# Attention inside a macaron block: maxima ahead of scores in the first half of each group of three turns, behind them in the second, with projections and transposes at other places in the order

## The reference

```
x = x + 0.5 * ffn(layernorm(x))
x = x + attention(layernorm(x))
x = x + 0.5 * ffn(layernorm(x))

ffn(x):        8 routed experts (top 2, normalized sigmoid gates) and one shared one,
               each gelu(x @ W1 + b1) @ W2 + b2, hidden size 128
attention(x):  its own layernorm with scale and bias gives h
               c_q = h @ w_down_q.T      c_kv = h @ w_down_kv.T      (128 wide)
               q, k, v = up-projections of c_q, c_kv, c_kv: 16 heads of 64
               rotary embedding on all 64 dimensions of q and k
               out = softmax(q k.T / 8) v @ w_out.T + x
```

## Time and profile before

| | |
|---|---|
| Median of 3 runs | 4095.67 us (4092.33 to 4099.59) |
| Profiled execution, its own time | 4098.04 us |
| Span in the profile | 4096.1 us, mean granted TensorE clock 0.988 |
| TensorE busy | 3897.4 us, 95% |
| GpSimd busy | 2932.8 us, 72% |
| VectorE busy | 2849.5 us, 70% |
| ScalarE busy | 2536.2 us, 62% |

### The profile page before, as it was taken

One profiled execution on the slowest core, in us unless ns is written; L12 is line 12 of the kernel. 1 busy time (PEld: TensorE's weight loads), 2 busy tenths in 40 slices (PEclk: granted clock), 3 DMA queues, 4 the chain that ended last, 5 costly groups with the idle time before them and its releaser, 6 DMA issues. The chain is left out here.

```text
span 4096.1 us, 65749 instructions
## 1 busy us (share of the span) xinstructions
PE 3897.4 (95%) x24908; PEld 2207.7 (54%) x24908; DVE 2849.5 (70%) x3796; ACT 2536.2 (62%) x3191; POOL 2932.8 (72%) x1632
## 2 busy tenths in 40 slices
PE   7999979999999999999999999999999999989999
PEld 6888834444444444444444444444444444478888
DVE  5656567777777776777778777767776777565563
ACT  4455446766766676667666766766676666645544
POOL 3444448878877897888788878878887888634443
PEclk9999989999999999999999999999999999999999
DMA  3233221111211221121122212211211121142331
GB/s 123 99 124 109 81 93 53 60 55 59 83 53 53 71 66 53 61 81 53 53 66 76 63 53 66 68 50 60 86 55 53 58 79 62 33 145 76 125 114 63
DMA packets 192772, 300.36 MB, mean 73 GB/s; under 512 B 50328, under 2 KB 100937, under 8 KB 191817
## 3 DMA queue, kind: packets, MB, share of 16 engines
q1 hardware_dynamic: 192456, 296.17, 22.3%
HBM read 201.20 MB, written 26.73 MB: 56 GB/s over the span
## 5 line engine op out<-in xcount | busy, mean ns | idle before, releaser
L1088 DVE TENSOR_REDUCE atNM<-atPS 128x2 f32<-128x1024 f32 x1024 | 1225.7, 1219 | 452.8 <-PE atPS L899 450.1
L1029 ACT ACTIVATE atPT<-atPS 128x1024 f32<-128x1024 f32 x1024 | 1014.0, 1024 | 773.1 <-PE atPS L920 766.7
L1187 POOL TENSOR_TENSOR atACC<-atACC,atPT 128x1024 f32<-128x1024 f32 x510 | 1238.7, 2429 | 89.3 <-ACT atPT L1029 39.1
L931 PE MATMUL atPO<-atPT,atV 128*64 128x512 f32 x4096 | 1014.2, 602 | 0.0
L1187 POOL TENSOR_TENSOR atACC<-atPT 128x1024 f32<-128x1024 f32 x255 | 606.6, 2379 | 262.8 <-PE atOT L953 181.7
L1020 ACT ACTIVATE atPS<-atSH 128x1024 f32<-128x1024 f32 x683 | 687.4, 1023 | 50.8 <-DVE atNM L1088 34.0
L920 PE MATMUL atPS<-atQH,atKL 64*128 64x512 f32 x2048 | 459.9, 445 | 66.3 <-DVE atPS L1094 51.7
L931 PEld LDWEIGHTS atPO<-atPT,atV 128*64 128x64 f32 x4096 | 259.0, 136 | 456.5 <-issue 433.1
L899 PE MATMUL atPS<-atKH,atQH 64*128 64x512 f32 x2048 | 444.0, 431 | 10.0 <-ACT atQH L1009 7.9
L1094 DVE COPY atPS<-atSH 128x1024 f32<-128x1024 f32 x341 | 418.7, 1228 | 37.9 <-DMA atSH<-atMD 11.4
L920 PE MATMUL atPS<-atQH,atKH 64*128 64x512 f32 x2048 | 406.6, 393 | 0.0
(11 more groups left out here) (278 smaller groups left out, 6461.5 us busy)
## 6 DMA issues: line engine op xcount, KB each, us to landing
atSH<-atMD SPq DMA_DIRECT2D x128, 512.0 KB, 4.3
atVT<-atR SPq DMA_DIRECT2D x508, 128.0 KB, 2.1
f1GB<-f1GD SPq DMA_DIRECT2D x128, 256.0 KB, 6.7
f2GB<-f2GD SPq DMA_DIRECT2D x128, 256.0 KB, 6.8
atRSUM<-atRD SPq DMA_DIRECT2D x126, 256.0 KB, 4.0
X<-x SPq DMA_DIRECT2D x4, 1024.0 KB, 6.0
XS<-x SPq DMA_DIRECT2D x16, 256.0 KB, 3.6
x<-X SPq DMA_DIRECT2D x16, 256.0 KB, 2.3
```

The lines of the kernel that those rows point to most:

```text
L931: ins = pe.eng.matmul(PO[HI[h], :], V[n % 2][:, j, HI[h]], PT[k % NPT][:, h, :], start=j == 0, stop=j == T - 1)
L1029: act.eng.activation(PT[k % NPT][:, :, :], PS[ring.of[step]][:, :, :], ACT.Exp, scale=SCALE).then_inc(grown.sem)
L1088: dve.eng.tensor_reduce(NM[:, q // 4, :, q % 4, t], PS[ring.of[step]][:, :, :], AX.X, ALU.max, negate=True).then_inc(most_out.sem)
L1187: pool.eng.tensor_tensor(total[:, :, :], begun[:, :, :], PT[k % NPT][:, :, :], ALU.add).then_inc(gathered.sem)
```

## The change

The order is written otherwise, in four respects; no instruction is added or taken away.

1. In the first half the maximum of turn x comes ahead of the score of turn x; in the second half the score of turn x+2 comes ahead of the maxima of turns x+1 and x+2. By TensorE's blocks: score, maximum, score and maximum, score, maximum become maximum, score, score and score, maximum, maximum. The ring of banks still gives each score the bank of the same maximum as before.
2. Where the side steps of turn x hold no other use of TensorE (`uses` is empty), those of turn x+1 are taken into the first half too, ahead of its attends.
3. Where turn x+1 has a `raise` and turn x+2 has another use, `apart` puts the steps of turn x+2 into the raise's place, ahead of the attends, and the raise behind the attends. That meets the raise of turn 4 with the sum of turn 5 (group 3), and in some batches a raise with a transpose or with the row of turn 11.
4. The transposes and latents of the second half of a batch's tokens stand at other periods (`TURNS`): transposes on turns 7 and 9 and not on 14 and 15, latents on 15 and 1 and not on 0 and 1.

```
-            TURNS = [(-21, late), (-20, late), (-17, early), (-17, late), (-9, early), (-9, late), (-8, early), (-8, late)]
+            TURNS = [(-21, late), (-20, late), (-17, early), (-17, late), (-13, late), (-12, late), (-9, late), (-8, late)]
...
+            def uses(steps):
+
+                return [s for s in steps if s[0] in ("turn", "latent", "raise", "value", "row", "sum", "outward")]
+
+            def apart(one, two):
+
+                raised = [s for s in one if s[0] == "raise"]
+                if raised and uses(two):
+                    return [s for s in one if s not in raised] + two, raised
+                return one, two
...
             for x in range(-42, 2 * PER * (NN + 4), 3):
-                order += tile("score", x) + most_of(x) + tile("fill", x + 2) + tile("score", x + 1)
-                order += others_of(x) + held + tile("attend", x - 1)
-                order += gathers(held + tile("attend", x - 1))
-                order += most_of(x + 1) + tile("score", x + 2) + most_of(x + 2)
+                order += most_of(x) + tile("fill", x + 2) + tile("score", x) + tile("score", x + 1)
+                now, some, more = held + tile("attend", x - 1), others_of(x), []
+                if not uses(some):
+                    more = others_of(x + 1)
+                order += some + more + now + gathers(now)
+                order += tile("score", x + 2) + most_of(x + 1) + most_of(x + 2)
                 now, held = tile("attend", x), tile("attend", x + 1)
                 if x % T < T - 1:
                     now, held = now + held, []
-                order += tile("fill", x + 3) + others_of(x + 1) + tile("fill", x + 4) + now + gathers(now) + others_of(x + 2)
+                one, two = apart(others_of(x + 1), others_of(x + 2))
+                order += tile("fill", x + 3) + one + tile("fill", x + 4) + now + gathers(now) + two
```

## The result

The changed kernel takes 4132.65 us (median of 4 runs, 4131.02 to 4133.29), the one before took 4097.14 beside it (4 runs, 4092.33 to 4099.59). The ratio is 1.0088, with a 95% interval of 1.007 to 1.0105. The forecast was 4099 with a range of 4065 to 4132, and slower was its likeliest sign at 0.40. The time lies at the range's upper edge, 0.65 us outside, and 34 us from the forecast. The profiled execution has a span of 4129.1 us, 33.0 more than before.

What follows compares the result with a forecast made beforehand. TensorE, 95% busy, was taken as the bound, with only its idle time to win. Losses of 5.5 and gains of 4.8 us per 96 turns gave +7.5, edit 4 -5, together +2.5: 4099 us, range 4065 to 4132.

Steps and rivals of the forecast that it cites:

- The sum for the hand-followed chains: Attention's two half-group chains, each group type followed once: 5.5 us lost, 4.8 won in 96 turns, +7.5 us in all.
- with `qlow` as in the row: Group 3: `qlow` taken at 1.9 to 2.2 us, group then 9.0 instead of 10.34, gain put at 1.1 each.
- the second rival: Group 3's `qlow` caught inside a GpSimd gather, 3.0 us each, and group 1's delaying group 4: +26, 4125; chance 0.14.
- -0.7 for each of the 7 batches, -5 in all: Edit 4's moved transposes: fewer waits behind `outward` (12.4 us), less ScalarE's copies and raises behind; between -12.4 and +5.
- B: Start of a group's third score, from which the second half's times are counted; 1818.56 in the group 7 followed.
- The loss list of 5.5 in 96 turns: Groups 7 (1.4), 2 and 10 (1.4), 11 (0.8), 13 without `outward` (0.5), smaller pieces in seven groups (1.4).
- the gains of 4.8: Per 96 turns: group 3 2.2 us, first halves with one attend and free VectorE (14, 15, 0, 1) 2.6.
- Only the gains come: Rival: second half's fill ready as before, losses of groups 7, 13, 2, 10 more than halved; 4062, chance 0.18.
- Bare second halves cost more than their row: Rival: ScalarE's own steps ahead of the late fill cost groups 12, 9, 5, 6, 8 0.3 each; +32, 4131; chance 0.13.
- the 20 that would have proved the sum wrong: Sign: score waits on ScalarE's fill rise from 12.8 to over 40 us; staying under 20 would disprove the sum.

## Why the prediction was wrong

**The sum for the hand-followed chains held in most of its parts.** It had 5.5 us lost and 4.8 won in 96 turns, +7.5 us in all; the groups without a transpose show +14.5, and group 3 below is 5 of the 7 between. Its largest losses are there by size: group 7 0.67 each (forecast 0.7), groups 2 and 10 0.25 to 0.45 (0.35), group 11 0.38 (0.4), group 13 without `outward` 0.42 (0.5). Of the gains, group 14 has 0.87, group 0 with `outward` 0.93, groups 1 and 15 0.48 and 0.47, as forecast (0.4 to 0.9). Group 1 with `outward` loses 0.22 and the other group 15 0.52, against 0.15 to 0.35.

**Group 3 was over-sized.** Its 1.1 each would be 23 us over 21 groups; the traces show 17.9. The step that failed is "with `qlow` as in the row". `qlow` did not stay at 1.9 to 2.2 but rose from a median of 1.93 to 2.69 in these groups. In them the changed kernel's group 3 takes 9.57 us with a `qlow` of 2.69, 9.78 with 2.90 and 10.05 with 3.17: what `qlow` takes more, the group takes more, and carried down to the 2.19 of the forecast the same line gives 9.07 for its 9.0.

The Trainium skill (page "SBUF — State Buffer", section "Who interferes with whom") says that only the port pair which VectorE and GpSimd share makes them contend, as an exclusive lock. The traces agree. In the kernel before and in the changed one `qlow` takes 1.21 to 1.22 us when it meets no gather. When it starts more than 0.15 us before the end of a gather, it ends 1.08 to 1.09 us behind that end, in all 39 and 38 cases. The other way round holds too: a gather that starts inside `qlow` ends 2.2 to 2.3 us behind `qlow`'s end, where a gather alone takes 2.38. So the length of `qlow` is the rest of a gather and 1.08, and moving it ahead inside the gather could win nothing.

That is the second rival's mechanism, and it happened, at less than its price. Its sign was the median of all 64 `qlow`, over 2.4 us; that median is 1.657 us (1.716 before), because the longer `qlow` is in group 3 and in a few of the groups 1. Its second part is there as well. In three of 21 pairs `qlow` in group 1 rose from 1.22 to 3.0 us, and the group 4 behind each is 1.45 to 1.49 us longer than before.

**The step that made the miss is edit 4's, "-0.7 for each of the 7 batches, -5 in all".** The groups with transposes show +16.1 instead: 21 of the 30.5 us by which the span missed the forecast of +2.5. It priced edit 4's transposes, with the copy HT and the raise behind it, and what it priced was about right: 5.4 us by the rows, and 7.5 in the run where no row is moved. What it put at nothing is the `row` of turn 11, which edit 3 also moves, in the four groups 9 that have a transpose on turn 9. My text names it in the change and no sentence of the sum costs it. Those four groups are 15.6 of the 16.1. Two of them would be there without edit 4, two are its doing, which is why undoing edit 4 changed the time by 1.4 us only. The price of such a row could be had from the chain that the prediction had already written down: the reductions end at B + 3.60 and the next use can start at B + 1.36, which is 2.24 us with nothing left to run, and `minus` (0.16) behind them makes 2.40. It was 2.39, four times, and behind three of them the clock took some 1.5 us more each (4.1 to 4.4 against 2.7). Letting the row stay behind gave 10.4 us back.

**The second half's order costs more than the losses that were listed, and the rest gains less.** The loss list of 5.5 in 96 turns is 59 us, the gains of 4.8 are 51. Undoing the second half's order gave back 56.8 us in the groups without a transpose and 15.4 in the others, 79.6 in all by the medians; the rest of the change is worth 44. So the near-cancelling sum stood for two large effects, both real, and neither is the list that was written. Group 7's loss, 15 of the 59, was mostly edit 2's (0.49 of 0.67 by the run that leaves it out there), and groups 14 and 4 would have won more with the old order (0.69 and 0.65). That 59 and 51 stand near 80 and 44 is luck in part.

**The other rivals.** "Only the gains come" needed the first maximum of a second half reduced within 0.7 us of the score's start; its reduction starts at 1.24. "Bare second halves cost more than their row" gives 4131, next to the measured time, and that is a coincidence. It asks for 0.3 us more in each of groups 5, 6, 8, 9 and 12; their medians are 0.03, 0.23, 0.01, -0.17 and 0.14, some 5 us in all for its 32.

**What the profile was to show.** Right: sum waits under 8 us (2.9), new waits of raise and value on the row copy (11.3 us over some 42 groups, 0.27 each), group 7 with its follower 0.7 more. Wrong: score waits on VectorE's fill did not halve, since the new third score has no maximum ahead of it and waits in many groups (0.17 in the group 7 shown, 14.4 and 10.1 us in all over the groups 11 and 4); those on ScalarE's fill rose to 21.6 and not over 40, just above the 20 that would have proved the sum wrong; group 3 took 9.78 and not 9.0.

**The best kernel that came of it** keeps the changed first half, the sum ahead of the attends and edit 4, takes back the second half's order and the row's new place, and leaves edit 2 out in group 7: 4038.07 us, 1.45% below the kernel before (0.9841 to 0.9870) and 2.3% below the changed one. With its old first half in group 3 it takes 4039.53, no different by these runs.

**What stays open.** Edit 1's second half costs 120 us alone and 80 with the rest. The waits of the third scores in groups 3, 4, 7 and 9 (71.5 against 21.0 us) go with that, but how the order, edit 2 and edit 3 share it was not taken apart. And 2.4 us of the span difference lie at the ends of the attention. There the changed kernel's trace has the lower clock from 564.7 to 581.7 us, as the attention begins, behind a first row that waits 1.90 us, and the trace of the kernel before does not; what that costs was not tested.

## What to carry to other kernels

When a reordering is a sum of gains and losses that nearly cancel, price the parts as kernels of their own before giving up or accepting the whole: here a part that costs 80 us hid a gain of 44. A step that moves ahead of its cover must be priced by what it depends on: look up its producer, and if that is a chain that starts at the instruction just ahead of it, the whole chain becomes idle time. Here `qlow`, started inside a gather, ended 1.08 us behind the gather's end wherever it stood, so its price in a new place was to be read from GpSimd's timeline and not from its own row. A move rule that is written for one kind of step (the sum) catches others by the same condition (the row); list everything that the condition catches.

## What the runs showed of the hardware that had not been expected

A wait of 2.39 us of TensorE in mid attention can cost more than itself. After three of the four such waits the granted clock was at its lower level, 0.61 or 0.62 on the mean of the next 3.5 to 4.5 us, and a pair of attends took 3.26 us where it takes 1.94. After the fourth, of the same length and in the same place of the order, the clock stayed at 1.00. The kernel before does it too. Its six longest waits of a sum are 1.92 to 2.09 us; the lower level follows those at 1293, 2567 and 3417 us, and not those at 1006, 1145 and 2282. Windows behind two of 2.08 or 2.09, with the columns of the earlier trace rows:

```profile
1147.40:1151.40 4.00, 4.00 (x27) 1.76 (x24) 3.77 (x5) 2.62 (x5) 4.00 (x3) 1.00 0.00 0
1295.60:1299.60 4.00, 4.00 (x18) 1.62 (x14) 3.06 (x3) 2.05 (x2) 4.00 (x3) 0.65 0.00 0
```

The same wait is followed by 27 matmuls in one stretch of 4 us and by 18 in the other. What decides between them no run here shows.

The second thing is how `qlow` on VectorE and a gather on GpSimd went together. Each works on 128x1024 elements of SBUF tiles, and they took turns. `qlow` alone took 1.21 to 1.22 us; started inside a gather it took up to 2.98 us before and 3.26 in the changed kernel, ending 1.08 to 1.09 behind the gather every time. A gather of 2.38 us that started inside `qlow` took up to 3.3 us before.
